# Second layer's adjacency product, chunk by chunk, with the norm and the next layer's scores between its row tiles

## The chip, the cores and the metric

The kernel runs on one NeuronCore of a Trainium2 chip, as one program of four layers. The time is the device time of one execution in microseconds. The kernel before took 980.51 us (median of 3 runs, 979.06 to 985.01).

## What is computed

Four graph layers on 2048 nodes with 128 features. `x` is 2048 x 128, `adj` is 2048 x 2048, all float32. Each layer's result is added to `x`, and the sum is normalised over the features. The change touches the second layer, its norm, and the first step of the third layer, the scores:

```python
def _L1_gnn_ref(features, adj, neigh_W, lin_W):      # second layer
    h = features @ neigh_W.T
    deg = adj.sum(axis=1, keepdims=True) + 1.0
    h = adj @ h / deg
    z = jnp.concatenate([features, h], axis=-1) @ lin_W.T
    return z

def _L2_gnn_ref(h, adj, weight, a_l, a_r, b):        # third layer
    x = h @ weight
    el = x @ a_l
    er = x @ a_r
    mask = adj != 0
    scores = el[:, None] + er[None, :]
    attn = jnp.exp(jax.nn.leaky_relu(scores, negative_slope=0.2))
    ...

x = _layernorm(x + _L0_gnn_ref(...), axis=-1)
x = _layernorm(x + _L1_gnn_ref(x, adj, L1_gnn_neigh_W, L1_gnn_lin_W), axis=-1)
x = _layernorm(x + _L2_gnn_ref(x, adj, L2_gnn_weight, L2_gnn_a_l, L2_gnn_a_r, L2_gnn_b), axis=-1)
x = _layernorm(x + _L3_gnn_ref(x, adj, ...), axis=-1)
```

## The kernel before

The nodes are cut into 16 row tiles of 128 (`NT`) and, as columns, into 4 chunks of 512 (`NCH`, `CH`). `X` holds the features with nodes on the partitions, one 128 x 128 block per row tile. `XT` holds them transposed. `AT` is the whole transposed adjacency matrix, 16 row tiles by 2048 columns, loaded before the second layer. `PS` is the PSUM, 8 banks of 512 columns.

Each engine has a queue of its own and runs it strictly in the order in which the program was written. Semaphores with readable names tie them together: `x_ready` counts finished norm groups (four row tiles, that is one chunk of nodes), `l1_mm` finished chunks of the adjacency product, `l1_aev` their copies to SBUF, `l1_b` the neighbour products, `xt_mm` and `xt_ev` transposes and their copies, `l2_rb`, `l2_rbev`, `l2_v` and `l2_vec` the scores and what is made of them. No scheduler reorders anything.

The second layer on TensorE (`later_pe`), before:

- For each chunk of nodes, `x_transpose(q)` transposes four tiles of `X` (L198) and `features(q)` multiplies with `neigh_W` (L654, in `tiles_product`), with ScalarE's copies between them (`xt_copy`, `evac`, L266).
- `adjacency_product(hj, q, l1_mm)` takes row tiles 4q to 4q + 3 and, inside them, all four column chunks: 16 f32 matmuls of 512 columns (L646). It is called four times; chunk c adds up in bank c. All four chunks end together, after the last row tile. Between the second and third call stands the product of `x` with the first half of `lin_W` into banks 4 to 7.
- Four neighbour products (L654) with the second half of `lin_W`, each after ScalarE's copy of its chunk.
- Four rounds of the third layer's start: transposes of the new `X` (L198, into bank q), a product of `XT` with a broadcast weight vector (L717), and four products of two columns (L720) for the per-node scores.

VectorE (`norm(1, ...)`) adds the scaled neighbour product to `X` (L970), takes mean and variance (L960, L963), has ScalarE take the root (`root`, L389, function Sqrt), inverts it (L947) and rescales (L949). It works one chunk behind: chunk q's rescale comes after chunk q + 1's sum. ScalarE makes `right_factor(q)`, exponentials of the scores (L429), and from the score columns three small exponentials (L443). VectorE then builds the masked attention weights, two passes per row tile (L1046, L1049), and TensorE multiplies them (L742).

ScalarE's functions come in table sets; a load (ACT_TABLE_LOAD) stands where the next function is in another set. Sqrt is not in the set that has Exp and Ln.

One f32 matmul shows as two records, each with a weight load of its own (PEld).

## Time and profile before

| | before |
|---|---|
| median of 3 runs | 980.51 us (979.06 to 985.01) |
| profiled execution | 980.19 us |
| its span, first to last instruction | 978.4 us |
| mean granted TensorE clock | 0.941 |
| TensorE / VectorE / ScalarE / GpSimd busy | 854.8 / 701.0 / 501.5 / 231.8 us |
| second layer, first adjacency record to start of the attention product | 484.97 to 581.99 us |

Times in rows are microseconds from the span's start unless marked ns. L646 is line 646 of the kernel. A timeline row gives start, length, engine, line, operation, output<-inputs, shapes, number of instructions merged, and in brackets the idle time before it with the instruction that ended it. PE is TensorE, PEld its weight loads, DVE is VectorE, ACT is ScalarE. PEclk is the granted clock, 1.00 being 2.4 GHz and 0.50 being 1.2 GHz.

### The profile page before, as it was taken

To read this page: it belongs to the slowest core of one execution; us is meant where nothing else is said; L and a number is where in the kernel's file an instruction comes from. 1 tells how busy PE (TensorE), PEld (TensorE's weight loads), DVE (VectorE), ACT (ScalarE), POOL (GpSimd) and SP (SyncE) were. 2 spreads that over 40 slices of the span, in tenths; PEclk is the share of its full clock that TensorE was granted. 3 is DMA by queue.
4 is the path that set the end of the run, shared out by engine and by line. 5 is a ranking of instruction groups with operands and counts; after the bars stand their busy time and mean duration, and the time that the engine had idled before them with its cause. 6 is when DMAs were issued, how large, how long until landed. Compare 5 with 4: busy or idle time off the path is not lost. (4 is left out here: it accounts for less than half of the span.)

```text
span 978.4 us, 11073 instructions
## 1 busy us (share of the span) xinstructions
PE 854.8 (87%) x3812; PEld 551.3 (56%) x3812; DVE 701.0 (72%) x1024; ACT 501.5 (51%) x758; POOL 231.8 (24%) x127
## 2 busy tenths in 40 slices
PE   4999943999999999999599889979689899898756
PEld 4755412888888888854355569944233343343323
DVE  3687739999999999527831348871287788789896
ACT  2755205777777777535210146503465665666531
POOL 5000000000000000000000010001497767778981
PEclk9999985999999999999799959999889999999988
DMA  8789755201220121069100000000331321323110
GB/s 266 258 294 367 274 224 219 87 10 77 86 86 12 74 86 43 0 245 423 46 0 1 1 0 1 1 0 22 121 119 57 118 76 57 119 76 121 54 65 11
DMA packets 38281, 102.62 MB, mean 105 GB/s; under 512 B 5584, under 2 KB 10586, under 8 KB 31322
## 3 DMA queue, kind: packets, MB, share of 16 engines
q1 hardware_dynamic: 36592, 101.84, 28.4%
q10 hardware_dynamic: 1648, 0.27, 0.2%
q8 instruction: 21, 0.34, 0.1%
q14 instruction: 20, 0.16, 0.0%
HBM read 83.97 MB, written 18.14 MB: 104 GB/s over the span
## 5 line engine op out<-in xcount | busy, mean ns | idle before, releaser
L1510 PE MATMUL PS<-big 128*128 128x256 f32 x768 | 193.9, 384 | 4.2 <-ACT big L1358 4.1
L198 PE MATMUL PS<-ident,big 128*128 128x128 f32 x1123 | 158.7, 282 | 40.4 <-DVE big L1687 29.1
L198 PEld LDWEIGHTS PS<-ident,big 128*128 128x128 f32 x1123 | 138.4, 146 | 65.6 <-issue 47.6
L360 POOL TENSOR_TENSOR big<-big 128x1024 f32<-128x1024 f32 x64 | 149.3, 2350 | 16.1 <-DMA big<-b_dram 8.2
L1510 PEld LDWEIGHTS PS<-big 128*128 128x128 f32 x768 | 133.5, 190 | 22.4 <-ACT big L1358 7.9
L845 PE MATMUL PS<-big,ident 128*128 128x512 f32 x256 | 128.3, 642 | 17.5 <-DVE big L1142 17.5
L1358 ACT ACTIVATE big<-PS 128x512 f32<-128x512 f32 x192 | 104.8, 598 | 58.5 <-PE PS L198 57.7
L1131 DVE TENSOR_TENSOR_SCAN big<-PS,stripes,big 128x512 f32<-128x512 f32 x96 | 117.0, 1263 | 8.1 <-ACT PS L558 7.7
L558 ACT ACTIVATE PS<-big,stripes 128x512 f32<-128x512 f32 x128 | 85.7, 685 | 63.2 <-DVE big L1131 63.0
L1687 DVE SCALAR_TENSOR_TENSOR big<-big,rz 128x2048 f32<-128x2048 f32 x48 | 112.7, 2350 | 0.9
L329 POOL MEMSET big<- 128x16 f32 x1 | 0.1, 132 | 477.7 <-DVE big L949 477.7
L1665 DVE CUSTOM_DVE_ANT_0 big<-big 128x2048 f32<-128x2048 bf16 x48 | 109.7, 2289 | 0.1
L1348 ACT ACTIVATE big<-big,ymin 128x2048 f32<-128x2048 f32 x48 | 96.3, 2006 | 25.2 <-DVE ymin L1665 24.9
L845 PEld LDWEIGHTS PS<-big,ident 128*128 128x128 f32 x256 | 52.6, 207 | 81.2 <-issue 58.0
L266 ACT ACTIVATE big<-PS 128x512 f32<-128x512 f32 (+2 forms) x42 | 24.1, 592 | 100.3 <-PE PS L646 43.3
L756 PE MATMUL PS<-big 128*128 128x512 f32 x128 | 63.3, 629 | 5.3 <-DVE big L949 5.3
L371 POOL TENSOR_TENSOR big<-big 128x1024 f32<-128x1024 f32 x23 | 54.1, 2351 | 37.7 <-DVE big L1131 37.6
L1142 DVE TENSOR_TENSOR big<-PS,big 128x1024 f32<-128x1024 f32 x41 | 49.5, 1207 | 18.6 <-PE PS L826 9.2
L742 PE MATMUL PS<-big 128*128 128x129 f32 x512 | 59.7, 281 | 1.1 <-DVE big L1049 1.1
L742 PEld LDWEIGHTS PS<-big 128*128 128x128 f32 x512 | 59.4, 197 | 1.4 <-issue 1.4
L646 PE MATMUL PS<-big 128*128 128x512 f32 x128 | 58.4, 617 | 1.5 <-DVE big L1013 0.9
L1448 PE MATMUL PS<-big 128*128 128x512 f32 x128 | 58.1, 596 | 0.0
(189 smaller groups left out, 979.0 us busy)
## 6 DMA issues: line engine op xcount, KB each, us to landing
big<-in_adj SPq DMA_DIRECT2D x16, 2048.0 KB, 8.4
at_dram<-big SPq DMA_DIRECT2D x4, 4096.0 KB, 17.1
big<-at_dram SPq DMA_DIRECT2D x4, 4096.0 KB, 27.4
big<-b_dram SPq DMA_DIRECT2D x16, 1024.0 KB, 5.0
big<-e_dram SPq DMA_DIRECT2D x6, 1024.0 KB, 13.9
big<-b_dram SPq DMA_DIRECT2D x23, 256.0 KB, 5.3
out_x<-big SPq DMA_DIRECT2D x4, 256.0 KB, 2.5
big<-in_L_gnn_conv_w SPq DMA_DIRECT2D x1, 512.0 KB, 4.5
```

The lines of the kernel that those rows point to most:

```text
L198: return nc.tensor.transpose(PS[:, bank, col:col + P], src, ident[:])
L360: nc.gpsimd.tensor_tensor(dbu[k % 3], du[c % 2], bb[group % 2][:, k % 4, :].unsqueeze(1).to_broadcast([P, DI, CH]), ALU.mult).then_inc(dbu ...
L558: nc.scalar.activation(PS[:, 5 + j % 3, :], dt_[c % 2][:, b, :], ACT.Exp, scale=na[:, b, n:n + 1]).then_inc(da_ready, 1)
L742: m = nc.tensor.matmul(sums(it, slice(0, P + 1)), q2[jt % 4][:, it * P:(it + 1) * P], x2[:, jt, :], start=(jt == 0 and it % 3 == 0), stop= ...
L756: m = nc.tensor.matmul(PS[:, bank, :], X[:, jt, :], AT[:, jt, c * CH:(c + 1) * CH], start=(jt == 0), stop=(jt == NT - 1))
L845: m = nc.tensor.matmul(PS[:, 2 + b, :], ident[:], v[:, b, :], start=False, stop=(n == STATES - 1))
L1131: nc.vector.tensor_tensor_scan(hs[k % 3][:, b, :], PS[:, 5 + j % 3, :], dbu[k % 3][:, b, :], state[:, n, b:b + 1] if c else 0.0, ALU.mult, ...
L1348: e = nc.scalar.activation(w[s], w[s], ACT.Exp, bias=ymin[:, s:s + 1], scale=-1.0, accum_out=zsum[:, s:s + 1])
L1358: nc.scalar.activation(qt[v % 4], PS[:, v % 4, :], ACT.Copy).then_inc(qt_ready, 1)
L1510: m = nc.tensor.matmul(PS[:, 4 + k // 3, 0:256], hw[:, jt, h, :], qt[v % 4][:, 256 * c:256 * c + 256], start=(h == 0 and jt == 0), stop=(h ...
L1665: m = nc.vector.tensor_tensor_reduce(out=w[s], in0=bm[2 * pair + j], in1=eb[:, 0, h, :], scale=1.0, scalar=3.0e38, op0=ALU.add, op1=ALU.mi ...
L1687: m = nc.vector.scalar_tensor_tensor(w[s], w[s], rz[:, s:s + 1], aw[pair][:, j, :], ALU.mult, ALU.mult)
```

## The change

The adjacency product goes chunk by chunk. Chunk 0 takes its row tiles 0 to 3, then, after the other chunks' transposes and feature products, 4 to 15. Chunks 1 to 3 follow, and between their groups of four row tiles stand the neighbour product of chunk c - 1 and, for c of 2 and 3, transposes and scores of chunk c - 2. On VectorE, the norm of this layer no longer works one chunk behind: each chunk is rescaled as soon as its root is there. On ScalarE, the inverse root of this norm and of the third layer's is made by Ln and Exp, so the reciprocal on VectorE goes, and the table set is loaded ahead of the layer.

```diff
--- before.py
+++ after.py
@@ -167,7 +167,7 @@
         l1_h, l1_hev, l1_mm = sem("l1_h"), sem("l1_hev"), sem("l1_mm")
         l2_mm, l2_rb, l2_rbev, ones_col = sem("l2_mm"), sem("l2_rb"), sem("l2_rbev"), sem("ones_col")
         l2_v, l2_vec, l2_x, l2_xev = sem("l2_v"), sem("l2_vec"), sem("l2_x"), sem("l2_xev")
-        gru_step = sem("gru_step")
+        gru_step, x_log = sem("gru_step"), sem("x_log")
         ones_ready, walb_ready, x_plus_b = sem("ones_ready"), sem("walb_ready"), sem("x_plus_b")
         q2_act, q2_ready, q2_used = sem("q2_act"), sem("q2_ready"), sem("q2_used")
         w2_in, w3_in, w4_in, cw_in = sem("w2_in"), sem("w3_in"), sem("w4_in"), sem("cw_in")
@@ -386,8 +386,13 @@
             def root(k, q):
 
                 act.wait_ge(var_ready, 4 * k + q + 1)
-                nc.scalar.activation(rstd[:, 4 * q:4 * q + 4], mv[:, 4 * q:4 * q + 4, 1], ACT.Sqrt,
-                                     bias=cst[:, 0:1]).then_inc(std_ready, 1)
+                cols = slice(4 * q, 4 * q + 4)
+                if k == 0:
+                    nc.scalar.activation(rstd[:, cols], mv[:, cols, 1], ACT.Sqrt, bias=cst[:, 0:1]).then_inc(std_ready, 1)
+                else:
+                    nc.scalar.activation(rstd[:, cols], mv[:, cols, 1], ACT.Ln, bias=cst[:, 0:1]).then_inc(x_log, 1)
+                    act.wait_ge(x_log, 4 * (k - 1) + q + 1)
+                    nc.scalar.activation(rstd[:, cols], rstd[:, cols], ACT.Exp, scale=-0.5).then_inc(std_ready, 1)
 
             def xt_copy(r, q, bank):
 
@@ -420,8 +425,7 @@
                 xt_copy(1, q, 4 + q)
             for q in range(1, 4):
                 evac(l1_h, q + 1, H1, q, 4 + q, l1_hev)
-            for q in range(4):
-                evac(l1_mm, q + 1, AHT, q, q, l1_aev)
+            nc.scalar.preload_act_table_set("natural_log_exp_and_others")
 
             def right_factor(q):
 
@@ -429,14 +433,15 @@
                 nc.scalar.activation(es[:, q * CH:(q + 1) * CH], PS[:, (5 + q) if q < 3 else 0, :], ACT.Exp,
                                      scale=0.8).then_inc(l2_rbev, 1)
 
-            root(1, 0)
-            for q in range(3):
-                xt_copy(2, q, q)
-                root(1, q + 1)
-            right_factor(0)
+            for q in range(4):
+                evac(l1_mm, q + 1, AHT, q, q, l1_aev)
+                if q < 3:
+                    root(1, q)
+                if q:
+                    xt_copy(2, q - 1, q - 1)
+                    right_factor(q - 1)
+            root(1, 3)
             xt_copy(2, 3, 3)
-            right_factor(1)
-            right_factor(2)
             right_factor(3)
             act.wait_ge(l2_v, 1)
             for dst, src, sc in ((bj, 1, 1.0), (dj, 1, 0.2), (ci, 0, 0.2)):
@@ -638,15 +643,15 @@
                     m = transpose_into(bank, b * P, src[:, 4 * q + b, :])
                 m.then_inc(xt_mm, 1)
 
-            def adjacency_product(weights, q, done):
-
-                pe.wait_ge(diag_back, q + 1)
-                for jt in range(4 * q, 4 * q + 4):
-                    for c in range(NCH):
-                        m = nc.tensor.matmul(PS[:, c, :], weights[:, jt, :], AT[:, jt, c * CH:(c + 1) * CH],
-                                             start=(jt == 0), stop=(jt == NT - 1))
-                        if jt == NT - 1:
-                            m.then_inc(done, 1)
+            def adjacency_product(weights, c, first, last, done):
+
+                for jt in range(first, last):
+                    if c == 0 and jt % 4 == 0:
+                        pe.wait_ge(diag_back, jt // 4 + 1)
+                    m = nc.tensor.matmul(PS[:, c, :], weights[:, jt, :], AT[:, jt, c * CH:(c + 1) * CH],
+                                         start=(jt == 0), stop=(jt == NT - 1))
+                if last == NT:
+                    m.then_inc(done, 1)
 
             def tiles_product(q, bank, left, right, done):
 
@@ -692,27 +697,28 @@
             x_transpose(0)
             features(0)
             pe.wait_ge(l1_hev, 1)
-            adjacency_product(hj, 0, l1_mm)
+            adjacency_product(hj, 0, 0, 4, l1_mm)
             for q in range(1, 4):
                 x_transpose(q)
             for q in range(1, 4):
                 features(q)
             pe.wait_ge(l1_hev, 4)
-            adjacency_product(hj, 1, l1_mm)
+            adjacency_product(hj, 0, 4, NT, l1_mm)
             for q in range(4):
                 tiles_product(q, 4 + q, XT, wt[:, 13, :], l1_a)
-            adjacency_product(hj, 2, l1_mm)
-            adjacency_product(hj, 3, l1_mm)
-            for q in range(4):
+
+            def neighbours(q):
+
                 pe.wait_ge(l1_aev, q + 1)
                 tiles_product(q, q, AHT, wt[:, 14, :], l1_b)
 
-            pe.wait_ge(w2_in, 16)
-            pe.wait_ge(walb_ready, 1)
-            pe.wait_ge(l1_add, 4)
-            for q in range(4):
+            def next_features(q):
+
                 pe.wait_ge(x_ready, 4 + q + 1)
                 xt_fill(2, q, q, X)
+
+            def next_scores(q):
+
                 pe.wait_ge(xt_ev, 8 + q + 1)
                 nc.tensor.matmul(PS[:, (5 + q) if q < 3 else 0, :], walb, XT[:, q * CH:(q + 1) * CH], start=True,
                                  stop=True).then_inc(l2_rb, 1)
@@ -721,6 +727,26 @@
                                          stop=True)
                 if q == 3:
                     m.then_inc(l2_v, 1)
+
+            for c in range(1, NCH):
+                adjacency_product(hj, c, 0, 4, l1_mm)
+                neighbours(c - 1)
+                adjacency_product(hj, c, 4, 8, l1_mm)
+                if c == 2:
+                    pe.wait_ge(w2_in, 16)
+                    pe.wait_ge(walb_ready, 1)
+                    pe.wait_ge(l1_add, 4)
+                if c >= 2:
+                    next_features(c - 2)
+                adjacency_product(hj, c, 8, 12, l1_mm)
+                if c >= 2:
+                    next_scores(c - 2)
+                adjacency_product(hj, c, 12, NT, l1_mm)
+            next_features(2)
+            neighbours(3)
+            next_scores(2)
+            next_features(3)
+            next_scores(3)
 
             def values(q):
 
@@ -944,17 +970,19 @@
 
                 def scale(q):
                     dve.wait_ge(std_ready, 4 * k + q + 1)
-                    link(nc.vector.reciprocal(rstd[:, 4 * q:4 * q + 4], rstd[:, 4 * q:4 * q + 4]))
+                    if k == 0:
+                        link(nc.vector.reciprocal(rstd[:, 4 * q:4 * q + 4], rstd[:, 4 * q:4 * q + 4]))
                     for i in range(4 * q, 4 * q + 4):
                         m = nc.vector.tensor_scalar(v[:, i, :], v[:, i, :], mv[:, i, 0:1], rstd[:, i:i + 1],
                                                     ALU.subtract, ALU.mult)
                     m.then_inc(ready, 1)
 
+                at_once = k == 1
                 for q in range(4):
-                    if q == 1:
+                    if q == 1 and not at_once:
                         scale(0)
                     residual(q)
-                    if q > 1:
+                    if q > 1 and not at_once:
                         scale(q - 1)
                     for i in range(4 * q, 4 * q + 4):
                         m = nc.vector.bn_stats(stats[:, i, :], v[:, i, :])
@@ -962,7 +990,10 @@
                     for i in range(4 * q, 4 * q + 4):
                         m = nc.vector.bn_aggr(mv[:, i, :], stats[:, i, :])
                     m.then_inc(var_ready, 1)
-                scale(3)
+                    if at_once:
+                        scale(q)
+                if not at_once:
+                    scale(3)
 
             def add_scaled(q, bank, factors):
```

The places that matter, as the programs stand in their queues ("waits" are the semaphores an instruction waits for). First TensorE at the start of the layer, before. L654 here are the feature products, L646 the adjacency product:

```order
L198 MATMUL PS<-ident,big 128x128 x3
L654 MATMUL PS<-wt,big 128x128 [waits xt_ev]
L654 MATMUL PS<-wt,big 128x128 x3
L646 MATMUL PS<-big 128x512 [waits diag_back,l1_hev]
L646 MATMUL PS<-big 128x512 x15
L198 MATMUL PS<-ident,big 128x128 [waits x_ready]
```

The same place in the change (line numbers are those of the changed kernel):

```order
L198 MATMUL PS<-ident,big 128x128 x3
L659 MATMUL PS<-wt,big 128x128 [waits xt_ev]
L659 MATMUL PS<-wt,big 128x128 x3
L651 MATMUL PS<-big 128x512 [waits diag_back,l1_hev]
L651 MATMUL PS<-big 128x512 x3
L198 MATMUL PS<-ident,big 128x128 [waits x_ready]
```

Four matmuls stand ahead of the next transposes instead of sixteen. Next TensorE at the end of the layer, before: last adjacency products, four neighbour products, first round of transposes and scores.

```order
L646 MATMUL PS<-big 128x512 x15
L654 MATMUL PS<-wt,big 128x128 [waits l1_aev]
L654 MATMUL PS<-wt,big 128x128 x3
...
L198 MATMUL PS<-ident,big 128x128 [waits l1_add,x_ready,walb_ready,w2_in]
L198 MATMUL PS<-ident,big 128x128 x3
L717 MATMUL PS<-big,wt 128x512 [waits xt_ev]
L720 MATMUL PS<-war,big 128x2 x4
L198 MATMUL PS<-ident,big 128x128 [waits x_ready]
```

And in the change, chunk 3 with what stands in it, to the last round:

```order
L659 MATMUL PS<-wt,big 128x128 [waits l1_aev]
L659 MATMUL PS<-wt,big 128x128 x3
L651 MATMUL PS<-big 128x512 x4
L198 MATMUL PS<-ident,big 128x128 [waits x_ready]
L198 MATMUL PS<-ident,big 128x128 x3
L651 MATMUL PS<-big 128x512 x4
L723 MATMUL PS<-big,wt 128x512 [waits xt_ev]
L726 MATMUL PS<-war,big 128x2 x4
L651 MATMUL PS<-big 128x512 x4
L198 MATMUL PS<-ident,big 128x128 [waits x_ready]
L198 MATMUL PS<-ident,big 128x128 x3
L659 MATMUL PS<-wt,big 128x128 [waits l1_aev]
```

Behind the last adjacency matmul stand now one neighbour product and two rounds, of which the first needs only a norm that is older. Last, ScalarE in the change around chunk 2 and 3 (L266 copies, L393 Ln, L395 Exp, L433 `right_factor`):

```order
L266 ACTIVATE big<-PS 128x512 [waits l1_mm]
L393 ACTIVATE rstd<-mv,cst 128x4 [waits var_ready]
L395 ACTIVATE rstd<-rstd 128x4 [waits x_log]
L266 ACTIVATE big<-PS 128x512 [waits xt_mm]
L433 ACTIVATE es<-PS 128x512 [waits l2_rb]
L266 ACTIVATE big<-PS 128x512 [waits l1_mm]
```

The exponential of a chunk's scores stands ahead of the next chunk's copy, where before all four copies came first.

## Rows read from the trace of the kernel before

**Rows 1.** The page: busy time of TensorE, and its clock in 40 slices.

```profile
PE 854.8 (87%) x3812; PEld 551.3 (56%) x3812; DVE 701.0 (72%) x1024; ACT 501.5 (51%) x758; POOL 231.8 (24%) x127
PEclk9999985999999999999799959999889999999988
```

**Rows 2.** Timeline of TensorE, from the layer's first adjacency product to its last.

```profile
484.97 16.76 PE L646 MATMUL PS<-big 128*128 128x512 f32 x32 [0.86 <-DVE big L1013]
501.57 1.47 PE L198 MATMUL PS<-ident,big 128*128 128x128 f32 x12
502.88 2.92 PE L654 MATMUL PS<-wt,big 128*128 128x128 f32 x24
506.49 14.00 PE L646 MATMUL PS<-big 128*128 128x512 f32 x32 [0.69 <-ACT big L266]
520.33 3.73 PE L654 MATMUL PS<-wt,big 128*128 128x128 f32 x32
523.90 27.63 PE L646 MATMUL PS<-big 128*128 128x512 f32 x64
```

**Rows 3.** Timeline of TensorE behind it, to the start of the attention product.

```profile
551.37 3.73 PE L654 MATMUL PS<-wt,big 128*128 128x128 f32 x32
556.82 0.63 PE L198 MATMUL PS<-ident,big 128*128 128x128 f32 x4 [1.72 <-DVE big L949]
558.13 1.39 PE L717 MATMUL PS<-big,wt 128*128 128x512 f32 x2 [0.69 <-ACT big L266]
...
571.91 1.09 PE L198 MATMUL PS<-ident,big 128*128 128x128 f32 x4
...
575.55 1.71 PE L720 MATMUL PS<-war,big 128*128 128x2 f32 x8
577.12 3.76 PE L654 MATMUL PS<-dgt,big 128*128 128x128 f32 x16
581.99 5.82 PE L742 MATMUL PS<-big 128*128 128x129 f32 x32 [1.11 <-DVE big L1049]
```

**Rows 4.** Timeline of ScalarE: last root of the first norm, the table load.

```profile
492.02 0.30 ACT L389 ACTIVATE rstd<-mv,cst 128x4 f32<-128x4 f32 x1 [3.27 <-DVE mv L963]
...
568.62 1.28 ACT L429 ACT_TABLE_LOAD   x1
569.92 0.60 ACT L429 ACTIVATE es<-PS 128x512 f32<-128x512 f32 x1
```

**Rows 5.** Timeline of VectorE: last rescale of the first norm, and the attention's first pass.

```profile
492.56 1.12 DVE L949 TENSOR_SCALAR big<-big,mv,rstd 128x128 f32<-128x128 f32 x4
...
577.66 1.74 DVE L1046 TENSOR_SCALAR big<-es,bj,dj 128x2048 f32<-128x2048 f32 x1 [7.70 <-ACT ci L443]
```

**Rows 6.** Stretches (start:end length, PE busy, PEclk, DMA share, GB/s).

```profile
490.00:491.00 1.00, 1.00 (x3) 0.70 0.00 0
558.00:559.00 1.00, 0.86 (x2) 0.93 0.00 0
586.00:587.00 1.00, 1.00 (x10) 0.92 0.00 0
```

**Rows 7.** Lines L646 and L756 (ns min/median/max), and the timeline of L1424.

```profile
L646 PEld LDWEIGHTS PS<-big x128: 186/190/338, 484.9 to 550.5; 128*128 128x128 f32 x128
L646 PE MATMUL PS<-big x128: 592/592/1190, 485.0 to 550.9; 128*128 128x512 f32 x128
L756 PE MATMUL PS<-big x128: 590/592/1130, 646.4 to 836.3; 128*128 128x512 f32 x128
38.30 3.63 PE L1424 MATMUL PS<-wa,big 128*128 128x6 f32 x32
```

**Rows 8.** Timeline of ScalarE: the one Sqrt of the last layer, a later Ln and Exp.

```profile
669.86 0.30 ACT L569 ACTIVATE rstd<-mv,cst 128x4 f32<-128x4 f32 x1 [1.37 <-DVE mv L1086]
...
707.73 0.30 ACT L489 ACTIVATE rstd<-mv,cst 128x4 f32<-128x4 f32 x1 [0.38 <-DVE mv L1086]
708.06 0.20 ACT L491 ACTIVATE rstd<-rstd 128x4 f32<-128x4 f32 x1
```

## The prediction

> **What bounds the kernel now.** The page first [rows 1]: TensorE is busy 854.8 us of 978.4, and its clock is at or near full except in a few slices. So time comes back only where TensorE waits, or runs at half clock, and only if its next work really starts earlier. Then its timeline through the second layer [rows 2, 3]. The long stretch, from 506.49 to 551.37, has no gap that matters: 96 matmul records of the adjacency product (two records to one f32 matmul) and 32 of the `lin_W` product. 32 records take 520.33 - 506.49 = 13.84 us, so 0.43 us each. Behind it TensorE is ragged: the neighbour product ends near 555.1, the first transposes wait 1.72 us for VectorE's norm, each score product waits 0.69 us for ScalarE's copy, and the scores end at 577.26. The attention product starts at 581.99, after ScalarE's three small exponentials and two VectorE passes [rows 3, 5].
>
> The clock explains half of that tail. The granted clock falls from full (2.4 GHz) to half (1.2 GHz) just before 559, after TensorE had idled 1.72 and 0.69 us, and returns at about 586.2 [rows 6]. So a round of transposes, score product and score columns took 577.26 - 571.91 = 5.35 us. It was half already at 484.97, when the layer's first product began (records of up to 1190 ns, twice the median [rows 7]), and rose at about 490.6. That is why those 32 records took 16.6 us instead of 13.84 [rows 2, 6].
>
> **The start of the layer, which gets worse.** Before, 32 records run while VectorE finishes the last norm tiles. Now only the 8 records of chunk 0 with row tiles 0 to 3 run ahead of the three transposes. At half clock (5.6 us of it at 0.86 us, the rest at 0.43) they end at about 491.4. Transposes of chunks 1 and 2 take 0.9 us, to 492.3. Chunk 3 needs the norm that ends at 493.68 [rows 5], so TensorE stands 1.5 us. From the start of the last four transposes to the next adjacency product before was 506.49 - (501.57 + 0.87) = 4.05 us [rows 2], ScalarE's copies included. ScalarE is free from 492.3 [rows 4], so that holds: 493.85 + 4.05 = 497.9. Then the 24 records not done yet: 24 x 0.4325 = 10.4 us, to 508.3. Before, the same work was done at 506.49. **Cost 1.8 us** at full clock. If the clock falls in the new gap it costs more; see the rivals.
>
> **The long stretch, which gets longer by what moves into it.** 44.9 us as before brings it to 553.2. Added, at full clock: three neighbour products of 8 records, 3.73 x 8/32 = 0.93 each [rows 3], 2.8 us; two chunks' transposes, 1.47 x 4/12, near 0.44 each, 0.9 us; two score products of 2 records at 0.43, 1.7 us; two sets of 8 narrow score records. Those were only seen at half clock in this place, but 32 of the same kind, with 6 columns, took 3.63 us early in the kernel at full clock [rows 7], so 0.91 each, 1.8 us. Together 7.2 us, end at **560.3**. I put no waits between them. Each moved step has 8 adjacency records, 3.45 us, in front of it. The longest chain under one of them is ScalarE's evacuation, 0.69 us as TensorE sees it. VectorE's norm of a chunk (5.45 us from the neighbour product's start to the transposes, 551.37 to 556.82) has more than a whole chunk. If that cover failed, the excess would appear as TensorE idle in front of the transposes, at most 5.45 - 3.45 = 2 us twice.
>
> Two things could spoil the dense rate. The old order used one weight tile for four chunks in a row, the new one changes it each time. But the old one already had 128 weight loads for 128 records [rows 7]; nothing was shared. And all matmuls in a row now add into one PSUM bank. The later product does exactly that already, and its records have the same median 592 ns [rows 7]. Cost nothing; both rows exclude a loss above some ns.
>
> **The new tail.** At 560.3, chunk 3 of the product is done. ScalarE evacuates it while chunk 2's transposes run, and the neighbour product starts 0.7 us later, at 561.0. 5.45 us on, the last norm is ready: 566.45. Under it lie chunk 2's scores. One round is left. I take it at half clock, 5.35 us, since in the trace smaller gaps than the coming one (about 2.7 us) went before the fall at 559: **571.8**, where it was 577.26. **Gain 5.4 us**, all the terms above included. At full clock the round would be 0.44 + 0.69 + 0.86 + 0.91 = 2.9 us.
>
> **Small edits.** Sqrt and reciprocal become Ln and Exp. Sqrt's start to the rescale was 492.02 to 492.56, 0.54 us [rows 4, 5]. Ln's start to Exp's end is 0.53 us at the place that already does it [rows 8]. Zero, also for the third layer's norm, which uses the same helper. The table load of 1.28 us that sat before the first score exponential [rows 4] moves to before the layer, off the path. Sqrt is still used once, at the first chunk of the last layer, and now needs a load there. ScalarE idles 1.37 us ahead of it [rows 8], and the load can go as soon as the engine is idle, ahead of the wait: exposed 0, at most 1.3 us. The Trainium skill (ScalarE: Activation LUTs, What ACT_TABLE_LOAD costs) counts 2.66 us for a switch, with a drain; by that the sum would be 1.3 us worse. The trace disagrees so far: the next operation started 1.30 us after the load began.
>
> On ScalarE's queue, a score exponential now stands ahead of the next chunk's evacuation. It waits for a score product that TensorE has issued 4 row tiles earlier, so it is done in time. GpSimd's bias add waits for the last copy and starts some 5 us sooner, with VectorE's first pass beside it as now. VectorE has nothing queued behind its norm waits but this layer's work. No DMA is added, and the weight that SP loads for this layer is long there.
>
> **The sum.** 980.19 (profiled execution) - 5.4 = 974.8. The median of the runs stands 0.3 above that execution, so 975.1; I forecast **975 us**. 1% is 9.8 us, about what a measurement of this kernel can tell from no change, so this is within 1%.
>
> **Rivals.**
> - *The clock stays or comes back early* in the tail. For it: the tail is 11.5 us now, not 26. Then the round gives back 2.45 us more, and the attention product starts at full clock, where it lost half of 586.2 - 582.0, 2.1 us. Against it: the fall at 559 after lesser gaps. **970.5**, chance 0.20. The Trainium skill (TensorE: Matmul & The Clock Gate, Loop structure matters more than you think) speaks for this one: with output tiles in the outer loop, another engine's copy-out "doesn't break PE warmth", long DMA waits do. Here waits for VectorE and ScalarE alone preceded the fall, so row and rule differ, and I go by the row.
> - *The clock falls at the start.* The gap of 1.5 us at 492.3 comes 2 us after the rise. If it falls, 24 feature records at half clock take 5.6 us (16 such took 3.76 [rows 3]) and not 2.9, and the product needs 5.6 us again to get the clock back, 2.8 us lost: +5.5, **980.5**. Chance 0.20.
> - *Slower: it falls there and does not come back.* The mechanism is in the trace: half clock for 27.3 us, 559 to 586.2, though TensorE worked through nearly all of 571.91 to 580.88 [rows 3]. The same from 494 on costs 13.7 us: 975 + 13.7 = **988.7**. It decides from 10.8 us of half clock on, where the gain of 5.4 is used up. Against it: 512-column products of this kind got the clock back in 5.6 us. Chance 0.05.
> - *It does not do what it says*: chunk c's chain is longer than its cover, and the dense stretch opens at each moved step. The bound above, 4 us, leaves 979. Chance 0.05.
>
> **The numbers.** Forecast 0.50, within 972.5 to 978. The range that holds 8 in 10 takes in half of the 970.5 case, that of 979, and nearly all of 980.5, and some us for the last layer, whose clock also dips and may dip elsewhere: **969.5 to 982**. Faster by over 1% (below 970.7) needs the first rival with luck: 0.12. Slower by over 1% (above 990.3) needs the third and more: 0.03. Within 1%: 0.85.
>
> **What would show it.** TensorE: next adjacency product at about 498 after the start; the last adjacency record ending at 560; the last transposes near 566.5; the attention product's start at 576 to 577, not 582. A loss of the moved work's cover shows as idle time of TensorE before transposes and neighbour products, released by VectorE or ScalarE. The granted clock between 494 and 505 and between 563 and 586 decides between the cases. I am wrong if TensorE's first matmul of attention moves by less than 2 or more than 9 us, or if the last layer changes its length by more than 3 us.

## The result and the profile after

The change is faster: 972.06 us (median of 7 runs, 968.36 to 973.04) against 979.35 us (7 runs). The ratio is 0.9911, 95% interval 0.9884 to 0.9937. In a second series it was 0.9931 (0.9908 to 0.9953). So the gain is 7.3 and 6.8 us, under 1%; forecast were 5.4 us and 975. The median lies in the range (969.5 to 982), but just below the band of the forecast itself (972.5 to 978).

The profiled execution after took 968.36 us, span 966.5, the fastest of its kernel and 11.8 us below the profiled one of before. Not all of that is the change. The first product of the GRU, in front of everything that was changed, stands in a row of before and in one after (timeline of TensorE: start, length, engine, line, operation, output<-inputs, shapes, count, idle before and what ended it):

```profile
428.07 1.12 PE L670 MATMUL PS<-ns,wt 128*128 x2 [1.27 <-DVE big L981]
```

```profile
425.62 1.12 PE L675 MATMUL PS<-ns,wt 128*128 x2 [1.27 <-DVE big L1012]
```

2.45 us were gone before the change begins. Over 13 profiles this instruction starts between 425.5 and 433.1, with the same code ahead of it. The spread is there in full much earlier: the transposes that wait some 29 us for VectorE start at 163.42 before and at 161.00 after, and between 160.87 and 168.45 in all 13. I therefore count from the GRU's first product. The table has, for each profile, the time from it to the attention product's first matmul, from there to the last layer's first product, to the first convolution product, and to the end of the span:

| kernel | to attention | attention | third norm and chunk 0 | rest |
|---|---|---|---|---|
| before | 153.9 | 64.4 | 27.1 | 304.8 |
| before_again | 154.6 | 64.2 | 27.1 | 303.9 |
| change | 148.3 | 64.0 | 26.7 | 301.9 |
| after_again | 147.8 | 62.6 | 26.7 | 304.0 |
| no_lnexp | 148.1 | 62.6 | 27.1 | 304.2 |
| order_only | 156.4 | 62.8 | 26.7 | 301.7 |
| v01 | 147.8 | 64.6 | 26.7 | 304.8 |
| v0123 | 147.8 | 62.5 | 26.7 | 303.4 |
| v0123_pool | 146.6 | 62.1 | 26.7 | 302.2 |
| v0123_pool_start | 144.5 | 61.4 | 26.7 | 304.8 |
| nb_only | 148.3 | 64.1 | 26.7 | 301.7 |
| pool_late | 147.5 | 64.0 | 26.7 | 303.3 |
| nb_pool | 146.2 | 64.0 | 26.7 | 303.7 |

Read down the columns. The first is the layer: 154.3 to 148.1 (means of two profiles each), 6.2 us. The third steps by 0.4 us and has no spread: that is Ln and Exp in the third norm. The last runs from 301.7 to 304.8, and the change itself has 301.9 and 304.0, so the 3 us that the first pair of profiles differ there are not shown to be the change's. The attention column spreads too (62.6 and 64.0 for the change); it is taken up below.

The layer in the change, on TensorE, from its first adjacency product; it answers to [rows 2, 3]:

```profile
483.61 6.09 PE L651 MATMUL PS<-big 128*128 128x512 f32 x8 [0.69 <-ACT big L266]
489.54 1.04 PE L198 MATMUL PS<-ident,big 128*128 128x128 f32 x8
491.29 0.66 PE L198 MATMUL PS<-ident,big 128*128 128x128 f32 x4 [0.71 <-DVE big L976]
491.79 2.84 PE L659 MATMUL PS<-wt,big 128*128 128x128 f32 x24
495.32 10.57 PE L651 MATMUL PS<-big 128*128 128x512 f32 x24 [0.69 <-ACT big L266]
505.72 3.73 PE L659 MATMUL PS<-wt,big 128*128 128x128 f32 x32
...
554.04 3.68 PE L651 MATMUL PS<-big 128*128 128x512 f32 x8
557.55 0.60 PE L198 MATMUL PS<-ident,big 128*128 128x128 f32 x4
558.40 1.16 PE L659 MATMUL PS<-wt,big 128*128 128x128 f32 x8 [0.25 <-ACT big L266]
559.40 1.02 PE L723 MATMUL PS<-big,wt 128*128 128x512 f32 x2
560.26 0.95 PE L726 MATMUL PS<-war,big 128*128 128x2 f32 x8
563.82 1.12 PE L198 MATMUL PS<-ident,big 128*128 128x128 f32 x4 [2.61 <-DVE big L976]
565.62 2.08 PE L723 MATMUL PS<-big,wt 128*128 128x512 f32 x2 [0.69 <-ACT big L266]
567.49 1.71 PE L726 MATMUL PS<-war,big 128*128 128x2 f32 x8
569.06 3.76 PE L659 MATMUL PS<-dgt,big 128*128 128x128 f32 x16
573.91 5.39 PE L768 MATMUL PS<-big 128*128 128x129 f32 x32 [1.09 <-DVE big L1080]
```

The reader is to see three things. Between 505.72 and 557.55 no row carries an idle time in brackets: all that moved in is covered. Behind it one wait is left, 2.61 us for the last norm. And the last round still takes 5.4 us, since the clock fell in that wait (at 563.6). Busy time and clock of stretches (start:end, length, busy time of PE, PEld, DVE, ACT, POOL, PEclk, DMA share, GB/s), the stretch without a gap:

```profile
505.72:557.55 51.83, 51.83 (x181) 27.77 (x180) 13.25 (x52) 5.69 (x13) 0.00 (x0) 1.00 0.00 1
```

and the seconds in which the clock turns (PE alone), answering to [rows 6]:

```profile
488.00:489.00 1.00, 1.00 (x3) 0.77 0.00 0
563.00:564.00 1.00, 0.18 (x1) 0.78 0.00 0
577.00:578.00 1.00, 1.00 (x10) 0.90 0.00 0
```

Half clock lasted 27.3 us in the tail of before and 13.6 here. In the second profile of the change it fell later, 0.9 us after the same wait of 2.61 us had ended, and half clock lasted 6.8 us. The load for the one Sqrt of the last layer, on ScalarE, answers to [rows 8]: it fits the gap, and Sqrt starts 1.37 us after the engine came free, as before.

```profile
659.00 0.58 ACT L488 ACTIVATE PS<-PS 128x512 f32<-128x512 f32 x1 [2.40 <-PE PS L792]
659.60 1.28 ACT L574 ACT_TABLE_LOAD   x1
660.95 0.30 ACT L574 ACTIVATE rstd<-mv,cst 128x4 f32<-128x4 f32 x1
```

### The profile page after: what moved, and what is told of

Same layout as the page of the kernel before. It is cut to its first block and busy times, and to the rows that moved or that the text cites. A ratio compares the mean times of both kernels' runs of the same rounds, so it can differ in the third digit from the quotient of the medians.

```text
span 966.5 us, 11071 instructions
## 1 busy us (share of the span) xinstructions
PE 847.7 (88%) x3812; PEld 547.0 (57%) x3812; DVE 698.3 (72%) x1016; ACT 503.7 (52%) x766; POOL 231.7 (24%) x127
## 5 line engine op out<-in xcount | busy, mean ns | idle before, releaser
L266 ACT ACTIVATE big<-PS 128x512 f32<-128x512 f32 (+2 forms) x42 | 24.1, 592 | 64.8 <-PE PS L651 24.0
```

## The experiments

**after_again** is the changed kernel, unedited.

> The changed kernel unchanged, beside the others. Theory: its gain over the kernel before is 5.5 us in the second layer (GRU's end to attention's start 105.8 us before, 100.2 in the first profile of the change) plus 0.4 us in the third norm, plus 0.5 us of half clock; the 2.45 us ahead of the layer and the 3 us of the last layer by which that profile was shorter too are run-to-run spread. Expected median 6 to 7 us below the kernel before, near 972.5; a profile whose attention product starts 5.5 us earlier after the GRU's end, but whose start of that layer and whose last layer are within 1.5 us of the kernel before. Rival: the last layer is really shorter by 3 us (its clock dips fall elsewhere): then it is 309.5 to 310 us again against 312.7.

973.07 us, ratio 0.9931 (0.9908 to 0.9953). To attention 147.8 us, in the rest 304.0. Theory held in the median, the layer and the last layer; the rival on the last layer fell. One part was missed: the product of the GRU started at 431.6, so the start of the program spreads by more than the 1.5 us that I gave it.

**before_again** is the kernel before, unedited.

> The kernel before, unchanged, for a second profile. Theory (what differs outside of the second layer and the third norm is spread): from the GRU's first product to the first adjacency record and on to attention's start 153.9 us again within 1 us; the last layer from its first convolution product to the end, 304.8 us in the first profile, anywhere from 301.5 to 305; GRU's first product anywhere from 425.5 to 431.6. Rival (the change shortens the last layer): 304.8 us again, and the change's profiles stay at 302 to 304.

Ratio 1.0014 (0.9982 to 1.0046); 154.6 and 303.9 us. Theory held.

**order_only**: the loop order without the interleaving.

```diff
             for c in range(1, NCH):
-                adjacency_product(hj, c, 0, 4, l1_mm)
-                neighbours(c - 1)
...
+                adjacency_product(hj, c, 0, NT, l1_mm)
+            for q in range(4):
+                neighbours(q)
...
+            for q in range(4):
+                next_features(q)
+                next_scores(q)
...
-                at_once = k == 1
+                at_once = False
```

ScalarE's queue is back in the old order too; Ln and Exp stay.

> Chunk-outer adjacency product alone: all four chunks complete, then neighbour products and the four rounds of transposes and scores behind it, with the norm one chunk behind, as in the kernel before; Ln and Exp kept. Theory (the gain is the moved work, not the loop order): the long stretch ends near 553 instead of 551.4 because of the shorter cover at the start, the tail of 26 us at half clock is back, total 1 to 2 us slower than the kernel before less 0.4 for the third norm: ratio 1.000 to 1.002, 979.5 to 981. Rival (the order itself, or one bank at a time, is faster): 974 or less.

976.96 us, ratio 0.9984 (0.9959 to 1.0009): under the 979.5 to 981 expected, as a ratio just under 1.000 to 1.002, and not told from the kernel before. But the time to attention was 156.4 us, 2.2 longer than the mean of before; the rest of this profile was at the short end. The long tail is back (552.07 to 581.99, 29.9 us; before 30.6), but only 17 us of it were at half clock (563.4 to 580.5) and not 26. Some 3 us are lost at the start (33.6 us from the layer's first transposes to the end of chunk 0's 32 adjacency records, before 30.3 and 31.0), and the tail gives 0.7 back. That start shows what I had named as a rival, in two rows of its timeline, with the row behind them and the second in which the clock turns:

```profile
488.36 0.65 PE L198 MATMUL PS<-ident,big 128*128 128x128 f32 x4 [1.78 <-DVE big L968]
491.24 0.70 PE L198 MATMUL PS<-ident,big 128*128 128x128 f32 x4 [2.23 <-DVE big L968]
491.74 4.47 PE L660 MATMUL PS<-wt,big 128*128 128x128 f32 x24
```

```profile
491.00:492.00 1.00, 0.76 (x6) 0.86 0.00 0
```

TensorE stood 1.78 and 2.23 us, the clock went to half, and the feature products took 4.47 us instead of 2.84. The waits were longer here because the first adjacency records ran at full clock (3.67 us for 8, in the change 6.09) and ended sooner, while VectorE's norms came no earlier. The loop order alone gives no gain that the median shows; it makes the rest possible.

**nb_only**: only the neighbour products, and with them the norms, between the row tiles; all four score rounds behind.

```diff
                 adjacency_product(hj, c, 4, 8, l1_mm)
...
-                if c >= 2:
-                    next_features(c - 2)
-                adjacency_product(hj, c, 8, 12, l1_mm)
-                if c >= 2:
-                    next_scores(c - 2)
-                adjacency_product(hj, c, 12, NT, l1_mm)
...
+                adjacency_product(hj, c, 8, NT, l1_mm)
             neighbours(3)
...
+            for q in range(4):
+                next_features(q)
+                next_scores(q)
```

ScalarE's copies and exponentials for the scores stand behind its copies of the chunks again.

> The change with only the neighbour products between the row tiles; all four rounds of transposes and scores stand behind the last neighbour product, as in the kernel before. Theory (the gain comes from the first three norms being done early, so that nothing waits for them; where the scores stand matters little, since the tail must wait 5.5 us for the last norm anyway): the long stretch ends 4.4 us earlier than in the change, three rounds of 2.9 to 3.2 us fill the wait, the last round follows without a wait; from the GRU's first product to attention's start 146 to 148.5 us (change 148.1, before 154.2). Rival (the scores had to move under the dense stretch): 150 to 153 us, since the clock falls in the rounds' waits of 0.7 us and each takes 5.2 us.

971.7 us, ratio 0.9966 (0.9935 to 0.9996), other runs of before than above. To attention 148.3 us: the same as the change. Its tail on TensorE:

```profile
554.09 1.16 PE L659 MATMUL PS<-wt,big 128*128 128x128 f32 x8 [0.69 <-ACT big L266]
555.08 0.60 PE L198 MATMUL PS<-ident,big 128*128 128x128 f32 x4
556.37 1.12 PE L723 MATMUL PS<-big,wt 128*128 128x512 f32 x2 [0.69 <-ACT big L266]
...
564.33 0.64 PE L198 MATMUL PS<-ident,big 128*128 128x128 f32 x4
565.65 1.13 PE L723 MATMUL PS<-big,wt 128*128 128x512 f32 x2 [0.69 <-ACT big L266]
566.61 0.95 PE L726 MATMUL PS<-war,big 128*128 128x2 f32 x8
567.42 2.03 PE L659 MATMUL PS<-dgt,big 128*128 128x128 f32 x16
573.94 5.45 PE L761 MATMUL PS<-big 128*128 128x129 f32 x32 [4.49 <-DVE big L1073]
```

The rounds take 3.1 us each at full clock, and none waits for a norm. So the part of the change that earns the time is the neighbour product of finished chunks, which starts the norms early. Whether scores stand in the dense stretch or fill the wait for the last norm made no difference to the start of attention. The rival (150 us and more) fell. That the two come out equal is in part chance: the scores end 1.7 and 1.2 us sooner after the layer's first transposes than in the two profiles of the change, and VectorE's first pass, 3.39 us long here, takes that back (see v01). The median's interval reaches from no gain to the change's gain, so this rests on one profile. nb_only keeps VectorE's norm at once as well; no run takes that alone away, so the neighbour product and the prompt norm are shown only together.

**no_lnexp**: Sqrt and reciprocal in both norms again.

```diff
-                if k == 0:
-                    nc.scalar.activation(rstd[:, cols], mv[:, cols, 1], ACT.Sqrt, bias=cst[:, 0:1]).then_inc(std_ready, 1)
-                else:
-                    nc.scalar.activation(rstd[:, cols], mv[:, cols, 1], ACT.Ln, bias=cst[:, 0:1]).then_inc(x_log, 1)
-                    act.wait_ge(x_log, 4 * (k - 1) + q + 1)
-                    nc.scalar.activation(rstd[:, cols], rstd[:, cols], ACT.Exp, scale=-0.5).then_inc(std_ready, 1)
+                nc.scalar.activation(rstd[:, cols], mv[:, cols, 1], ACT.Sqrt, bias=cst[:, 0:1]).then_inc(std_ready, 1)
...
-                    if k == 0:
-                        link(nc.vector.reciprocal(rstd[:, 4 * q:4 * q + 4], rstd[:, 4 * q:4 * q + 4]))
+                    link(nc.vector.reciprocal(rstd[:, 4 * q:4 * q + 4], rstd[:, 4 * q:4 * q + 4]))
```

> The change with Sqrt and reciprocal in the second and third layer's norms again, instead of Ln and Exp; Sqrt then alternates with Exp within the layer, so each switch needs a table load of 1.28 us. Theory (Ln and Exp are worth little): all loads but the last two lie under the adjacency chunks; the last two fall into ScalarE's waits of 1.0 and 2.2 us, so at most 0.3 us on the last norm and 0.4 us in the third norm: 0.3 to 1 us slower than the change. Rival (the loads are what the interleaving needed to lose): 2.5 us or more slower, with TensorE's wait for the last norm 1.3 us longer and its wait for the score exponentials too.

973.26 us, ratio 0.9913 (0.9884 to 0.9943). The wait for the last norm grew from 2.61 to 2.87 us, the third norm from 26.7 to 27.1. ScalarE's timeline has the two loads where they were expected:

```profile
564.32 1.28 ACT L390 ACT_TABLE_LOAD   x1
565.62 0.30 ACT L390 ACTIVATE rstd<-mv,cst 128x4 f32<-128x4 f32 x1
...
568.64 1.28 ACT L428 ACT_TABLE_LOAD   x1
570.78 0.60 ACT L428 ACTIVATE es<-PS 128x512 f32<-128x512 f32 x1 [0.86 <-PE PS L718]
```

Ln and Exp are worth 0.3 us in the layer and 0.4 in the third norm by these rows, 0.7 in all. The medians can't tell, and neither can the time to attention alone: 148.1 us, as the mean of the change. The Trainium skill (ScalarE: Activation LUTs, What ACT_TABLE_LOAD costs) adds a drain to each switch, 2.66 us in all; here the next operation starts 1.30 us after the load began.

**v01**: something for TensorE to do in the last wait.

```diff
             next_scores(2)
+            values(0)
+            values(1)
             next_features(3)
             next_scores(3)
...
-            values(0)
-            values(1)
```

> The change with the third layer's first two feature products (values 0 and 1, 16 records, 1.9 us at full clock) moved from behind the last scores into TensorE's 2.6 us wait for the last norm. Theory (half clock in the last round comes from that wait): the wait shrinks to about 0.8 us, the granted clock stays full through the last round, which takes 2.9 us and not 5.35; attention starts 2.4 us earlier, total 2 to 4 us below the change. Rival (the clock falls anyway, as it did at 559 in the kernel before after shorter waits, or falls in the now empty 5 us ahead of attention): last round 5.35 us, total within 0.5 us of the change.

971.09 us, ratio 0.9919 (0.989 to 0.9948). The first half of the theory held, the second did not:

```profile
566.24 0.66 PE L198 MATMUL PS<-ident,big 128*128 128x128 f32 x4 [0.72 <-DVE big L976]
567.58 1.12 PE L723 MATMUL PS<-big,wt 128*128 128x512 f32 x2 [0.69 <-ACT big L266]
568.54 0.95 PE L726 MATMUL PS<-war,big 128*128 128x2 f32 x8
575.87 5.96 PE L768 MATMUL PS<-big 128*128 128x129 f32 x32 [6.37 <-DVE big L1080]
```

The round was at full clock, 3.3 us, and ended 2.1 and 1.7 us earlier than in the two profiles of the change, counted from the layer's first transposes. Yet attention starts at the same 147.8 us. VectorE and GpSimd in the same profile:

```profile
569.90 3.38 DVE L1077 TENSOR_SCALAR big<-es,bj,dj 128x2048 f32<-128x2048 f32 x1 [3.71 <-ACT ci L448]
```

```profile
567.68 4.51 POOL L332 TENSOR_TENSOR big<-big,wt 128x2048 f32<-128x2048 f32 x1 [73.84 <-ACT big L266]
```

VectorE's pass takes 1.34 us elsewhere. Here it takes 3.38, and ends 1.09 us after GpSimd's bias add (572.19 to 573.28). In the change the same pass began 0.64 us before the add's end (570.25) and took 1.72:

```profile
569.61 1.72 DVE L1077 TENSOR_SCALAR big<-es,bj,dj 128x2048 f32<-128x2048 f32 x1 [5.84 <-ACT ci L448]
```

```profile
565.73 4.52 POOL L332 TENSOR_TENSOR big<-big,wt 128x2048 f32<-128x2048 f32 x1 [74.30 <-ACT big L266]
```

What was won on TensorE turned into a wait behind GpSimd.

**v0123**: in addition, the other two feature products ahead of attention.

```diff
             next_scores(3)
+            values(2)
+            values(3)
...
-                if jt == 0:
-                    for q in range(2, 4):
-                        values(q)
```

> As v01, and the other two feature products (values 2 and 3) moved from between the first and second row tile of attention to ahead of it, where TensorE waits for VectorE's first pass. Theory: 1.95 us of TensorE's work leave the attention stretch; its second row tile now waits for ScalarE's and VectorE's second pass by at most 0.5 us, since ScalarE starts it 2 us earlier: total 3.5 to 6 us below the change. Rival: attention is then bound by the passes in its first tiles, and the gain over v01 is under 0.5 us.

970.18 us, ratio 0.9925 (0.9898 to 0.9952): 147.8 and 62.5 us. Attention is 1.5 to 2 us shorter than in the change's first profile and in v01, but after_again reached 62.6 without it. Not settled; VectorE's pass was again 3.38 us.

**v0123_pool** and **pool_late**: the bias add held back until eight row tiles of attention weights are made, with and without the moved products.

```diff
             pool.wait_ge(xt_ev, 12)
+            pool.wait_ge(q2_ready, 8)
             nc.gpsimd.tensor_tensor(X, X, b2b...
```

> As v0123, and GpSimd's bias add on X (4.5 us) waits until eight row tiles of attention weights are made, instead of starting behind the last copy of the transposes. Theory (in v01 and v0123 VectorE's first pass took 3.38 us and not 1.34 because GpSimd's add ran until 1.1 us before its end): the pass takes 1.34 us, attention starts 2 us earlier after the last scores than in v0123 (6.4 us there), and later passes are delayed without TensorE waiting, since three tiles are made ahead: 1.5 to 2.5 us below v0123. Rival (the pass is slow for another reason, the granted state of its inputs or ScalarE's reads beside it): 3.38 us again.

969.61 us, ratio 0.9881 (0.985 to 0.9911).

```profile
574.94 1.35 DVE L1077 TENSOR_SCALAR big<-es,bj,dj 128x2048 f32<-128x2048 f32 x1 [3.72 <-ACT ci L449]
576.32 2.29 DVE L1080 SCALAR_TENSOR_TENSOR big<-big 128x2048 f32<-128x2048 f32 x1
```

The pass takes 1.35 us: the add was the cause. Attention started 1.3 us earlier, not 2, because now TensorE's own two products, at half clock since its wait of 1.54 us, ended last.

> The change with GpSimd's bias add waiting until eight row tiles of attention weights are made, nothing else. Theory: VectorE's first pass takes 1.34 us and not 1.7, attention starts 0.4 us earlier (147.7 us after the GRU's first product, change 148.1), no more, because at half clock in the last round the add was nearly over. Rival (the add delays more than the one pass): 1 us or more earlier.

970.34 us, ratio 0.9931 (0.9903 to 0.9959). 147.5 us to attention, the pass 1.35 us. Theory held: in the change the collision costs about 0.4 us. Against after_again, whose last round also began at full clock, the start of attention is 0.4 us earlier; against the first profile it is 0.8. The kernel before pays the same 0.4 us (its pass took 1.74), so this is no loss of the change.

**nb_pool** is nb_only with that wait.

> nb_only with the late bias add. Theory (with the last round at full clock the add costs 2 us, as v0123 against v0123_pool showed less clearly): attention starts 1.5 to 2 us earlier than in nb_only if its last round is at full clock, 0.4 us if at half clock: 144 to 147 us. Rival: no difference from nb_only.

971.74 us, ratio 0.9937 (0.9905 to 0.9968). 146.2 us, 2.0 less than nb_only, with the clock full from 493 us to the end of attention. The theory held in the profile; the median did not follow, within its interval. A part of the answer is in the attention column, 64.0 us in spite of the full clock: the add that was held back now meets a later pass, and TensorE waits 1.23 us for that pass, until 607.83.

**v0123_pool_start**: as v0123_pool, and the start filled.

```diff
-            for q in range(1, 4):
-                x_transpose(q)
+            x_transpose(1)
+            x_transpose(2)
+            adjacency_product(hj, 1, 0, 2, l1_mm)
+            x_transpose(3)
             for q in range(1, 4):
                 features(q)
+            adjacency_product(hj, 1, 2, 4, l1_mm)
             pe.wait_ge(l1_hev, 4)
...
-                adjacency_product(hj, c, 0, 4, l1_mm)
+                adjacency_product(hj, c, 4 if c == 1 else 0, 6 if c == 1 else 4, l1_mm)
                 neighbours(c - 1)
-                adjacency_product(hj, c, 4, 8, l1_mm)
+                adjacency_product(hj, c, 6 if c == 1 else 4, 8, l1_mm)
```

> As v0123_pool, and at the start of the layer two row tiles of chunk 1's product stand ahead of the third chunk's transposes and two behind the feature products, where TensorE waits for a norm (0.7 us) and for ScalarE's copy (0.7 us). Theory: 1.0 to 1.4 us earlier at the end of the long stretch. Rival (TensorE's waits there are longer than the profile of the change shows, since its first records run at half clock): no gain, up to 1 us lost.

967.61 us, ratio 0.9861 (0.9833 to 0.9889). The waits at the start are gone, the feature products run into the adjacency product without a bracket:

```profile
498.23 1.88 PE L652 MATMUL PS<-big 128*128 128x512 f32 x4
499.95 0.60 PE L198 MATMUL PS<-ident,big 128*128 128x128 f32 x4
500.39 2.84 PE L660 MATMUL PS<-wt,big 128*128 128x128 f32 x24
503.07 12.18 PE L652 MATMUL PS<-big 128*128 128x512 f32 x28
```

The transposes behind the last adjacency product came 82.5 us after the layer's first transposes (563.49 - 481.04), in v0123_pool 83.8 (565.01 - 481.17): 1.4 us, as expected. This version has the best ratio of all. Its interval lies clear below that of after_again (0.9908 to 0.9953) and overlaps the first one of the change (0.9884 to 0.9937) by 0.0005; the change was not run in the same series, and it has only 6 runs. What the filled start adds to v0123_pool is shown by the profiles alone, since those two intervals overlap.

## Why the prediction was right, and where a size was off

**The mechanism and the layer's sum** were right. Counted from the layer's first transposes on `ns` (476.15 before, 473.70 after), attention began after 105.8 us and 100.2: 5.6 us, forecast 5.4. Step by step:

- *Start, cost 1.8 us.* Four chunks' features and 32 adjacency records were done 30.3 us after those transposes before (476.15 to 506.49, [rows 2]), and 32.0 us after (473.70 to 505.72): 1.7 us. The single wait was 0.71 us and not 1.5: chunk 0's transposes and feature products ran at half clock (1.12 and 2.08 us, before 0.66 and 1.26), so the adjacency product began 9.9 us after the first transposes and not 8.8. The cost does not depend on it, since VectorE's last norm sets the start of the last transposes, 17.6 us after the first ones as forecast. In no_lnexp and pool_late the wait was 1.67 and 1.72 us, in after_again it was gone, and the same work took 32.0 us in all three. The forecast's end of the first 8 adjacency records, 491.4, should read 491.2 by its own terms; nothing hangs on it. The second profile of before took 31.0 us here, so the cost is 1.0 to 1.7 us.
- *Long stretch, 52.0 us* from chunk 0's end to chunk 3's. Measured 51.83 with TensorE busy for all of it. No loss from changing weight tiles or from one bank in a row.
- *Tail, 16.2 us* from there to attention (11.5 and the 4.7 us behind the last scores). Measured 16.36 and, in after_again, 15.9. The last round was at half clock as assumed.
- *Sqrt's load, nothing*: right.
- *Third norm, nothing*: wrong in size. I weighed Ln and Exp against Sqrt and reciprocal on the one chain and found them equal, and left it at that. But this norm still works one chunk behind, where the root is ready long before VectorE comes to it. There the reciprocal stood alone in VectorE's queue: TensorE's second and third wait for this norm are 1.13 and 0.66 us in the change, 1.34 and 0.87 before, 0.21 us each. 27.1 against 26.7 us, no_lnexp with 27.1: 0.4 us.
- *Attention, nothing*: the half clock after its start took 4.2 and 3.8 us in the two profiles of before, 3.3 and nothing in those of the change. The rival of the early clock came true in part and in some executions. By the attention column this is 0.4 to 1.8 us, and it is clock luck too: v01 and nb_only have 64.6 and 64.1.

5.6 to 6.2 in the layer, 0.4 in the third norm and 0.4 to 1.8 in attention make 6.4 to 8.4 us; the medians give 7.3 and 6.8. What is open is how much of the clock's share belongs to the change and how much to chance. Of the 2.9 us by which the median lies under 975, 1.2 come from the start of the sum: over 7 runs the kernel before has 979.35, not the 980.51 of 3 runs.

**The signs.** Attention's first matmul moved by 8.1 us, within the 2 to 9 allowed; with the 2.45 us ahead of the layer added back, it and the three marks before it stand within 0.3 us of the places forecast. The other sign of being wrong was met in the first pair: counted from its first product, the last layer went from 332.0 to 328.6 us, 3.4 shorter. In the second pair it is 331.1 and 330.8 us, no more than the third norm's 0.4 us apart, so I put the first pair's difference down to spread; two profiles of each do not prove it.

**The rivals.** The clock did not fall at the start of either profile of the change, nor in no_lnexp and pool_late, whose wait there was 1.7 us. It fell in order_only, and cost 1.6 us (4.47 against 2.84 us for 24 feature records) and not the 5.5 of the forecast, because it was back at full before the adjacency product, whose 24 records took 10.57 us as in the change. It fell in the tail, after 2.61 us of waiting for VectorE. The Trainium skill (TensorE: Matmul & The Clock Gate, Loop structure matters more than you think) names a long wait for DMA as what lets the clock fall, and lets another engine's copy-out pass; this wait was for VectorE, so row and page still differ. nb_pool, with no gap above 0.69 us until the scores' end, and then one of 2.44 us, kept full clock throughout. That it does not do what it says fell with 51.83 us busy out of 51.83.

**What I had not seen.** I named GpSimd's add "beside VectorE's first pass, as now" and priced it at nothing. The row was there: 1.74 us for the first pass [rows 5] against 1.34 for the later ones. It cost both kernels 0.4 us, and it takes up to 2 us from whoever improves the tail.

## What to carry to other kernels

Close a long reduction chunk by chunk when a chain on other engines hangs on its result, and start that chain at once; what else could move under the dense stretch matters only as far as the last chunk's chain leaves TensorE idle. To compare two profiles, count from an instruction ahead of the change, and look at a second profile of each before a difference far behind the change is explained. When a tail is shortened, look which engine's work was hidden in it: here an add on GpSimd took back 2 us of a VectorE pass.

## What the runs showed of the hardware

GpSimd's 4.5 us add and two kinds of VectorE pass did not share, they excluded each other. The pass with one large input ended 1.09 us after the add in v01 and 1.08 after it in the change, whether it had begun 2.3 or 0.64 us before the add's end (3.38 and 1.72 us instead of 1.34). When the add came in the middle of attention, it fell on the pass with two large inputs, in v0123_pool_start:

```profile
600.38 6.53 DVE L1083 SCALAR_TENSOR_TENSOR big<-big 128x2048 f32<-128x2048 f32 x1
```

```profile
599.27 5.49 POOL L333 TENSOR_TENSOR big<-big,wt 128x2048 f32<-128x2048 f32 x1 [100.51 <-DVE big L1083]
```

6.53 us instead of 2.29; it ended 2.15 us after the add. The add, too, took 5.49 us instead of 4.5: it began beside a one-input pass that ended at 600.34. TensorE worked on from tiles made ahead and waited 0.15 us; in pool_late and nb_pool the same meeting cost it 0.63 and 1.23 us. The Trainium skill (SBUF — State Buffer, Who interferes with whom) calls the port pair of the two an exclusive lock held for the whole instruction; these rows agree.

The first product of the GRU moved between 425.5 and 433.1 us for the same program ahead of it. That spread, which had arisen before 161 to 168.5 us, is as large as the effect under study. What makes it was not looked into.
